# One layer of graph attention, mixing and eight experts on one core: the experts' inner rows made turned, with W1 as the weights

## What is computed

```python
xn = layernorm(x)
x  = x + gnn(xn, src, dst) + mix(xn)      # graph attention with 4 heads; linear attention and a small MLP
x  = x + ffn(layernorm(x))                # 8 experts, each row goes to its best 2
# ffn, for each row and each of its two experts e:
#   h   = gelu(xn @ W1[e] + b1[e])        # 256 -> 512, the "inner row"
#   y_e = h @ W2[e] + b2[e]               # 512 -> 256
#   y  += y_e * w_full[e]
```

## Time and profile before

| what | value |
|---|---|
| median of 3 runs | 2148.51 us (2148.22 to 2149.25) |
| the profiled execution | 2151.45 us, of it 2149.7 us from the first to the last instruction |
| PE matmul busy | 1847.4 us (86% of the span), 9214 records |
| DVE busy | 1596.9 us (74%) |
| POOL busy | 1457.0 us (68%), of it 1347 indirect gathers: 1284.8 us |
| ACT busy | 1095.9 us (51%) |
| granted TensorE clock | 0.912 of full speed, as a mean |

### The profile page before, as it was taken

The page is one execution under the profiler, slowest core; times in us unless marked ns, Lnnn a source line. Parts: engine busy times, 40 slices in busy tenths (PEclk is TensorE's granted clock), DMA queues, the critical chain, the costliest instruction groups (busy, mean ns, idle before and its releaser), DMA issues. The chain is left out here.

```text
span 2149.7 us, 37968 instructions
## 1 busy us (share of the span) xinstructions
PE 1847.4 (86%) x9214; PEld 1342.0 (62%) x9215; DVE 1596.9 (74%) x3938; ACT 1095.9 (51%) x1953; POOL 1457.0 (68%) x1586
## 2 busy tenths in 40 slices
PE   8499998588677777767989999889999999998795
PEld 6367776466565555655666667666766777774463
DVE  7678887557787777779887888878878878854331
ACT  4433333235455555445666667666647676733121
POOL 3277777777777777777766777666777777725551
PEclk9799999888787777878999999999999999998898
DMA  9576665686666665666776777766687777736762
GB/s 332 145 192 178 175 168 154 205 266 188 173 180 180 175 179 171 179 166 180 203 205 189 212 211 215 228 195 172 193 248 203 208 203 189 189 91 220 229 208 64
DMA packets 289628, 411.64 MB, mean 191 GB/s; under 512 B 109299, under 2 KB 211987, under 8 KB 285694
## 3 DMA queue, kind: packets, MB, share of 16 engines
q0 software_dynamic: 74208, 206.08, 35.8%
q1 hardware_dynamic: 194988, 185.27, 28.7%
q10 hardware_dynamic: 20210, 17.79, 2.7%
HBM read 354.64 MB, written 91.00 MB: 207 GB/s over the span
## 5 line engine op out<-in xcount | busy, mean ns | idle before, releaser
L1556 POOL DMA_INDIRECT rows_g<-node_table,src_all x1347 | 1284.8, 954 | 485.6 <-issue 405.6
L2349 PE MATMUL psB<-rows_g,pick_e 128*128 128x260 f32 x2704 | 729.5, 430 | 123.2 <-issue 113.5
L2349 PEld LDWEIGHTS psB<-rows_g,pick_e 128*128 128x128 f32 x2704 | 571.2, 217 | 239.2 <-issue 139.3
L1731 DVE TENSOR_TENSOR rows_g<-rows_g,psD 128x2048 f32<-128x2048 f32 x169 | 384.7, 2276 | 0.0
L2141 ACT ACTIVATE pick_n<-local_row 128x1024 bf16<-128x1024 bf16 x169 | 178.6, 1057 | 228.0 <-PE psA L2338 216.7
L2390 PE MATMUL psC<-W_f,xnT 128*128 x476 | 237.9, 622 | 0.0
L1794 DVE COPY xn<-psD 128x256 f32<-128x256 f32 x119 | 50.2, 422 | 226.8 <-DMA set_dram<-xn 74.4
L1702 DVE TENSOR_TENSOR pick_e<-psD,slot_all 128x1024 f32<-128x1024 f32 x169 | 203.5, 1204 | 0.3 <-issue 0.2
L2137 ACT ACTIVATE local_row<-local_row,minus_id 128x1024 bf16<-128x1024 bf16 x169 | 191.5, 1133 | 13.0 <-DVE both_f L2041 8.7
L1578 POOL DMA_INDIRECT rows_g<-set_dram,places x98 | 95.0, 969 | 146.5 <-issue 106.6
L2338 PEld LDWEIGHTS psA<-window,pick_n 128*128 128x128 bf16 x1352 | 55.0, 99 | 141.6 <-issue 137.1
(11 more groups left out here) (388 smaller groups left out, 3021.3 us busy)
## 6 DMA issues: line engine op xcount, KB each, us to landing
local_row<-local_dram SPq DMA_DIRECT2D x169, 256.0 KB, 3.9
sent_dram<-sorted_dram SPq DMA_DIRECT2D x176, 128.0 KB
rows_g<-node_table,src_all POOLq DMA_INDIRECT x1347
xin<-sent_dram SPq DMA_DIRECT2D x119, 128.0 KB
xnT<-in_xT_dram SPq DMA_DIRECT2D x96, 128.0 KB
set_dram<-xn SPq DMA_DIRECT2D x87, 128.0 KB
sent_dram<-zero_dram SPq DMA_DIRECT2D x24, 384.0 KB
acc<-node_table SPq DMA_DIRECT2D x49, 128.0 KB, 3.5
```

The lines of the kernel that those rows point to most:

```text
L1556: pool.indirect_dma_start(out=rows_g[:, r, j], out_offset=None, in_=node_table, in_offset=bass.IndirectOffsetOnAxis(ap=src_all[:, g, j:j + ...
L1731: dve.tensor_tensor(heads, heads, p_here.unsqueeze(3).broadcast_to([P, EG, HEADS, C]), ALU.mult).then_inc(ph_ready, 1)
L2349: last = pe.matmul(ps_sum[s % 2][:, 0:AW], pick_e[:, s % SLOTS, j], rows_g[:, s % RING, j, 0:AW], start=(j == 0), stop=(j == EG - 1))
```

## The change

The inner rows of a block come out of PE turned.

- `up`, for a block: W1 in pieces of 128x128 is the weights now, and the block's turned rows (`xnT`, 128 columns) stream. That is four pieces times two halves: 8 products of 128 columns instead of 2 of 512. The result is 128 inner columns on the partitions and the block's 128 rows along the bank. There is no bias product.
- [...] `W1_now` has one buffer: the copy waits for the product of the block before.
- `gelu`, for a block: four activations of 128 columns from PSUM straight into the turned rows, each with the bias column of its expert and piece added (`inner_bias`, laid out by the host). `hid`, `turn_h` and `take_h` are left to the mixing jobs.
- Two banks are used in turn for the inner rows (`inner_bank`).
- The output product moves from step s+3 to s+2, DVE's copy from s+4 to s+3, the store likewise, and the last collects one step forward.
- Only the biases b2 go through the split, the DRAM table and back (one load less, three stores less).

```diff
-            hid = sb("hid", [P, H], c=ph)
+            hid = sb("hid", [P, D], c=ph)
+            W1_now = sb("W1_now", [P, KT, H], c=ph)
+            inner_bank = lambda n: (ps_up, ps_hT)[n % 2]
...
-        at = max([job_step[last_job[z]] + (5 if ends else 6)] + [c + 1 for c in final_at.values()])
+        at = max([job_step[last_job[z]] + (4 if ends else 5)] + [c + 1 for c in final_at.values()])
...
+                def take_weights(n, a, k):
+                    b = first_block[a] + k
+                    if k == 0:
+                        act.wait_ge(table_ready, 2 * (a + 1))
+                    if b == 0:
+                        act.wait_ge(weights_f, 16)
+                    experts[n] = act.value_load(blk_expert[0:1, b:b + 1], min_val=0, max_val=NE - 1)
+                    act.wait_ge(up_done, n)
+                    act.activation(W1_now[:].rearrange("p k n -> p (k n)"), W1_f[:, bass.ds(experts[n], 1)].rearrange("p e k n -> p (e k n)"),
+                                   ACT.Copy).then_inc(weights_taken, 1)
...
                     else:
+                        e = experts.pop(n)
+                        if first_block[a] + k == 0:
+                            act.wait_ge(inner_bias_in, 16)
                         act.wait_ge(up_done, n + 1)
-                        act.wait_ge(h_turned, n)
-                        act.activation(hid[:], ps_up[:, :], ACT.Gelu).then_inc(gelu_done, 1)
+                        act.wait_ge(down_done, n - 1)
+                        for c in range(HK):
+                            last = act.activation(turned_rows(n, kind)[:, c], inner_bank(n)[:, c * P:(c + 1) * P], ACT.Gelu, bias=inner_bias[:, bass.ds(e, 1), c])
+                        last.then_inc(hT_ready, 1)
...
-                        if jobs_with(s - 2):
+                        if jobs_with(s - 2) and jobs_with(s - 2)[1] == "mix":
                             take_h(*jobs_with(s - 2))
+                        if jobs_with(s) and jobs_with(s)[1] == "block":
+                            take_weights(jobs_with(s)[0], jobs_with(s)[2], jobs_with(s)[3])
                         if jobs_with(s - 1):
                             gelu(*jobs_with(s - 1))
...
-                        else:
-                            pe.wait_ge(gelu_done, n)
-                        pe.matmul(ps_up[:, :], bias_of[0:BR, bass.ds(e, 1)].rearrange("p o n -> p (o n)"), bias_parts[0:BR, 0:H], start=True, stop=False)
+                        pe.wait_ge(weights_taken, n - NT + 1)
+                        pe.wait_ge(hT_ready, max(n - 1, NT))
                         pe.wait_ge(xT_taken, turn_number[("job", n)] + 1)
-                        for c in range(KT):
-                            last = pe.matmul(ps_up[:, :], xnT[:, u, c], W1_f[:, bass.ds(e, 1), c], start=False, stop=(c == KT - 1))
+                        for c in range(HK):
+                            for k in range(KT):
+                                last = pe.matmul(inner_bank(n)[:, c * P:(c + 1) * P],
+                                                 W1_now[:, k, c * P:(c + 1) * P], xnT[:, u, k],
+                                                 start=(k == 0), stop=(k == KT - 1))
...
-                        if jobs_with(s - 2):
+                        if jobs_with(s - 2) and jobs_with(s - 2)[1] == "mix":
                             turn_h(*jobs_with(s - 2))
...
-                        if jobs_with(s - 2) and jobs_with(s - 2)[1] == "mix":
+                        if jobs_with(s - 2):
                             down(*jobs_with(s - 2))
-                        if jobs_with(s - 3) and jobs_with(s - 3)[1] == "block":
-                            down(*jobs_with(s - 3))
```

More of the change, by code:

```diff
@@ L195, in gps_layer @@
     final_number = {t: f for f, t in enumerate(final_at)}
[L196 removed]
+    assert max(final_at[t] for t in final_at if t not in tiles_in[-1]) < job_step[last_job[-1]] + 4
     sum_at = {t: final_at[t] + (4 if t in tiles_in[-1] else 2) for t in final_at}
@@ L1273, in small_writes @@
             def small_writes(s):
-                return (sum(1 for n, kind, _, _ in job_at.values() if job_step[n] + (2 if kind == "mix" else 3) < s), sum(1 for t in route_at if route_at[t] + 3 < s),
+                return (sum(1 for n, kind, _, _ in job_at.values() if job_step[n] + 2 < s), sum(1 for t in route_at if route_at[t] + 3 < s),
                         sum(1 for t in route_at if route_at[t] + 4 < s), sum(1 for at in table_at[:1] if at - 1 < s))
@@ L1501, in on_sync @@
                         job = jobs_with(c - 3)
[L1502 to L1505, removed]
+                        if job and (job[1] == "mix" or c - 3 < LATE):
                             store(*job)
@@ L2082, in on_vector @@
                         small_written(s)
-                        if jobs_with(s - 3) and jobs_with(s - 3)[1] == "mix":
+                        if jobs_with(s - 3):
                             result(*jobs_with(s - 3))
-                        if jobs_with(s - 4) and jobs_with(s - 4)[1] == "block":
-                            result(*jobs_with(s - 4))
                         for t in range(FULL, -1, -1):
@@ L2149, in gelu @@
                 def gelu(n, kind, a, k):
-                    rows, cols = (tile_rows(a), D) if kind == "mix" else (P, H)
                     if kind == "mix":
+                        rows = tile_rows(a)
                         act.wait_ge(hb_ready, n + 1)
-                        act.activation(hid[0:rows, 0:cols], hid[0:rows, 0:cols], ACT.Gelu).then_inc(gelu_done, 1)
+                        act.activation(hid[0:rows, 0:D], hid[0:rows, 0:D], ACT.Gelu).then_inc(gelu_done, 1)
                     else:
+                        e = experts.pop(n)
@@ L2159, in take_h @@
+                        last.then_inc(hT_ready, 1)
                 def take_h(n, kind, a, k):
-                    rows, parts = (tile_rows(a), KT) if kind == "mix" else (P, HK)
+                    rows = tile_rows(a)
                     act.wait_ge(h_turned, n + 1)
                     if n >= 1:
-                        act.wait_ge(down_done, n if kind == "mix" else n - 1)
-                    act.activation(turned_rows(n, kind)[:, 0:parts, 0:rows], ps_hT[:, 0:parts * P].rearrange("p (c n) -> p c n", c=parts)[:, :, 0:rows],
+                        act.wait_ge(down_done, n)
@@ L2165, in take_h @@
+                    act.activation(hidT[:, 0:KT, 0:rows], ps_hT[:, 0:KT * P].rearrange("p (c n) -> p c n", c=KT)[:, :, 0:rows],
                                    ACT.Copy).then_inc(hT_ready, 1)
@@ L2324, in on_scalar @@
                                 exponentials(x)
-                        if s - 5 >= LATE and jobs_with(s - 5):
-                            store(*jobs_with(s - 5))
+                        if s - 4 >= LATE and jobs_with(s - 4):
+                            store(*jobs_with(s - 4))
             def on_tensor(pe):
@@ L2397, in turn_h @@
                         pe.wait_ge(hT_ready, n)
-                    for c in range(parts):
+                    for c in range(KT):
                         last = pe.transpose(ps_hT[:, c * P:c * P + rows], hid[0:rows, c * P:(c + 1) * P], ident[0:rows, 0:rows])
@@ L2423, in down @@
                             pe.wait_ge(weights_2, 32)
-                        pe.matmul(ps_small[:, down_at], bias_of[0:BR, bass.ds(e, 1)].rearrange("p o n -> p (o n)"), bias_parts[0:BR, H:], start=True, stop=False)
+                            pe.wait_ge(bias_of_ready, 1)
+                            pe.wait_ge(bias_in, 16)
+                        pe.matmul(ps_small[:, down_at], bias_of[0:BR, bass.ds(e, 1)].rearrange("p o n -> p (o n)"), bias_parts[0:BR], start=True, stop=False)
                         for c in range(HK):
```

47 lines of the change are left out of this document (23 added, 24 removed).

## The result

The changed kernel takes 2122.06 us (median of 4 runs, 2116.04 to 2122.76); the kernel before, run beside it, 2148.36 (2145.76 to 2149.25). The ratio is 0.988 with an interval of 0.986 to 0.991. So it is 26 us faster, where 56 were forecast: the sign is right, the size is less than half. The time lies near that of rival A (2118), whose parts were 21 us for the steps with sums and 9 for the rest.

The account below looks back on a forecast made before the run. POOL's gathers were taken to bound the kernel until 1059 us, then PE within POOL's pace. From 2151.45 us, 42 for steps with sums and 14 for the tail gave 2095.5, 2092 on the runs' scale; range 2080 to 2106.

Parts of the forecast that it names:

- rival A: DVE and POOL hold the pace, so half the gain in steps with sums is lost: 2118 us, chance 0.22.
- PE's price of a block: Inner product on PE: 16 passes take 1.82 us, as before; without bias product and turns a block saves 0.76 us.
- Rival C: Weight loads on PE don't overlap: each block costs 1.0 us more, 2262 us, chance 0.03.
- ACT: ACT's work grows by 1.7 us a step, from 7.5 to 9.2, against POOL's 10.0.
- Rival B: ACT becomes the bound at +3.7 us a step, making the kernel slower: near 2212 us, chance 0.06.
- Steps 142 to 168: Steps with sums from 1626 us: pace falls to POOL's 10.0 us a step, 16 us gained before a clock discount.
- the clock: In steps with sums, PE's granted clock may fall when it waits for POOL; 3 us taken off the gain.
- Steps 82 to 141: Earlier steps with sums: gain of 22 us by 1357 us and 29 us by 1626 us.
- the pace of the gathers: POOL's eight gathers take 10.0 us, so no step with sums can be shorter than that in the mean.
- a clock below 1.00 from 1357 to 1626 us: Sign that would show the forecast right: PE's granted clock below 1.00 in that stretch of steps with sums.
- The tail: Steps without sums fall from 5.02 to 4.26 us; with limits from POOL and routing, 14 us gained together.
- Tail steps near 5 if PE waits for ACT's copy: Sign for steps without sums: 4.3 us if right; near 5 means PE waits for ACT's copy of W1.

Follow-up runs that it names:

- early stores: ACT issues the tail's stores at the head of its step; against the original kernel, 0.980 on the changed kernel, 0.997 on the original.
- both orders: Tail stores at the head of ACT's step, logits and count before the block's inner product; against the original kernel, 0.973 on the changed kernel, 0.988 on the original.

## Why the prediction was right or wrong

**PE's price of a block: right.** The 16 passes take 1.78 us (1.82 forecast), the whole saving is 0.88 us (0.76). 128 columns fit beside a load of weights as 65 did. The Trainium skill's rule ("TensorE: Matmul & The Clock Gate", "The mechanism"), by which loads overlap only with other row groups, doesn't hold for these passes: by it they would take 3.6 us. The same section also lets a load run ahead into a background weight buffer; no record here shows whether that is what happens. Rival C fell.

**ACT: right in kind, too dear.** +1.0 us a step (7.5 to 8.5) instead of +1.7: the four gelus last 1.14 us together and not 1.56, because each begins before the record of the last has ended. The load of the expert's number, put at 0.3 us, shows as 3.9 us of idle time before 25 copies, 0.16 each. While sums run, PE waited 1.3 us for `W1_now`, once. Rival B fell.

**Steps 142 to 168: right.** 18.5 us, where 16 less 3 for the clock were forecast. PE was the bound; the end gap of 15.4 us between gathers and sums is now 5.4, below the 6.5 that the prediction held for the least.

**Steps 82 to 141: the step that failed.** The prediction counted 22 us by 1357 us, with PE's waits for DVE at half, and 29 by 1626. Measured are 4.2 by the pick of step 116 and 9.6 by that of 142, one pair of executions; the pair with early stores shows 2.4 and -1.2. Already stood against the 22 us: from 1059 to 1357 us POOL had waited for only 17, and more could come from the reserve of gathered rows alone.

First, and shown: PE's saving there lay in DVE's shadow. In step 90 its sums began when they had before, and the whole saving became waiting. With 32 us less of PE work, the stretch takes as long (615.5 and 615.6 us with both orders), and with 26 us given back hardly longer. The sum counted a step's PE time as gain wherever PE didn't wait in that step. What sets the pace over several steps in after is the circle of DVE's chain and PE's logits and count; where that is shortened, it is POOL with DVE close behind.

Second, the pace of the gathers. The prediction named it, and took too little off for it. At the pick of step 136 after was 13.9 us ahead of before (4.9 and 4.5 us in the pairs with early stores and with both orders), at that of 142 still 9.6 (-1.2 and 0). In step 139 of after DVE waits 8.73 us for gathered rows and PE 5.7 us (3.0 in before), while POOL makes one gather every 1.25 us from 1564 to 1597 us without a real wait. At step 121 PE stands for 7.7 us instead of 5.8, for rows that come through DRAM. What these two stops would be at another pace of POOL was not tried.

Third, the clock. Slow sums took 22 us in excess in after and 12 in before, so 10 more, where I had put 3 for all the steps with sums; with filler they took 11. That this is time of the kernel isn't shown: with both orders the filler brought the excess from 17 to 9 us and left the time where it was (0.973 without, 0.975 with). The sign that the prediction gave, a clock below 1.00 from 1357 to 1626 us, tells nothing: it was 0.95 there before, and is 0.93 from 1350 to 1610 us.

Rival A named the mechanism, "DVE and POOL hold the pace", and should have had the larger chance for this stretch; the rows on which it rested, and the earlier trace rows, were at hand.

**The tail: the second miss.** PE's steps do fall to 4.14 us with early stores, and between kernels that have them the tail is worth 14 to 21 us, where 14 were forecast. In after it is worth 5 to 7. There the store stands behind `take_x` and the copy of W1 in ACT's order, and its circle, 9.65 us, is longer than two PE steps of 4.14 us, but was shorter than two of 5.02. The copy accounts for some 6 us of it. The prediction looked for a wait for ACT's copy in PE's `up`, where next to none is; it did not ask who stands behind the copy on ACT. "Tail steps near 5 if PE waits for ACT's copy" was right as a sign and wrong in its reading.

## What to carry to other kernels

Before you count an engine's saved time, look where in the step it lies: work between two waits for another engine can be free, and taking it away then buys nothing; let the circle across engines (here result, choice, products, sums, logits, count) set the step, not the busiest engine's row. An instruction added to an engine delays everything queued behind it, DMA issues first; put stores ahead of it. And test a faster engine by giving its work back as filler: if the time stays, it wasn't the bound.

## What the hardware did that was not expected

- Filler work kept the clock up: with 8 unused transposes in 16 steps the sums of step 90 took 3.75 us at a granted clock of 1.00, without them 6.46 us at 0.58. The kernel's time with it (0.986) is not told apart from that without (0.988).
- In step 90 the clock fell behind waits of 1.93 and 1.85 us with 0.8 us of work between them; behind waits of 0.98 and 1.42 us, with 1.3 us of work between, the sums kept their 3.75 us. But in step 87 the sums kept them too, behind waits of 1.75 and 1.85 us.
- 16 float32 passes of 128 columns with 16 different weights took 1.78 us, 0.111 each, no more than those of 65 and 4 columns.
- Four gelus of 128 columns in a row took 1.14 us, though each is recorded with 0.365.
